# Moving the digit block of VectorE, the high digits of ScalarE and the gate of GpSimd's index cells in a product-key layer pipeline

## The reference

```python
h = h + attention(layernorm(h))          # scores, softmax and values all from the same rows
h = h + ffn(layernorm(h))
# ffn, for each token and each of 8 heads:
q = layernorm(hidden @ Wq.T + bq) * ln_g + ln_b       # 64 values, two halves of 32
s0, s1 = l2norm(q0) @ l2norm(keys0).T, l2norm(q1) @ l2norm(keys1).T   # 64 scores each
sc0, ix0 = top_k(s0, 16); sc1, ix1 = top_k(s1, 16)
cs = sc0[:, None] + sc1[None, :]; ci = ix0[:, None] + ix1[None, :]    # 256 candidates
fs, pos = top_k(cs, 16); fi = ci[pos]; w = softmax(fs)
out = sum over heads and 16 picks of gelu(hidden . down[fi]) * w * up[fi]
```

## Time and profile before

| | |
|---|---|
| time, median of 3 runs | 2086.8 us (2083.2 to 2092.77) |
| profiled execution, its own time | 2086.99 us |
| its span | 2085.2 us |
| its mean granted TensorE clock | 0.77 |
| busy: PE, DVE, ACT, POOL | 1701.8, 1925.5, 1217.5, 1554.2 us |

### The profile page before, as it was taken

The page is one execution under the profiler, slowest core; times in us unless marked ns, Lnnn a source line. Parts: engine busy times, 40 slices in busy tenths (PEclk is TensorE's granted clock), DMA queues, the critical chain, the costliest instruction groups (busy, mean ns, idle before and its releaser), DMA issues.

```text
span 2085.2 us, 48099 instructions
## 1 busy us (share of the span) xinstructions
PE 1701.8 (82%) x11423; PEld 1296.2 (62%) x11423; DVE 1925.5 (92%) x15878; ACT 1217.5 (58%) x3851; POOL 1554.2 (75%) x2561
## 2 busy tenths in 40 slices
PE   5567888888889898898888898888988989788766
PEld 3335576756767576675667667565765757566556
DVE  3299999999999999999999999999999999999992
ACT  3345656666565566655566665666665556665454
POOL 2238787886878788787878868788787767878765
PEclk9676878768787777877788678876878777787666
DMA  1000000000000000000000000000000000000000
GB/s 35 13 9 2 19 7 8 20 6 19 6 19 7 6 19 9 19 6 18 8 6 19 9 17 9 13 12 6 19 7 19 9 9 16 7 13 9 6 6 11
DMA packets 46672, 24.86 MB, mean 12 GB/s; under 512 B 4955, under 2 KB 46116, under 8 KB 46390
## 3 DMA queue, kind: packets, MB, share of 16 engines
q1 hardware_dynamic: 46390, 21.80, 3.7%
HBM read 11.52 MB, written 10.26 MB: 10 GB/s over the span
## 4 chain that ended last, share of the span: by engine, by line
PE 38%; DVE 30%; ACT 16%; POOL 9%; issue 5%; SPq 0%; another core or an unknown queue 0%; DMA 0%; POOLq 0%; DVEq 0%; ACTq 0%
PE QB L531 8%; DVE alpha L1046 5%; PE FB L449 5%; PE FB L440 4%; PE SC L480 4%; ACT WD L732 4%; DVE idx L1030 4%; DVE idx L1033 4%; DVE hrest L1024 3%; PE QB L519 3%; ACT hi L672 3%; PE FB L421 3%; DVE vals L1028 2%; DVE vals L1021 2%; POOL sa L762 2%
## 5 line engine op out<-in xcount | busy, mean ns | idle before, releaser
L892 POOL TENSOR_TENSOR bw<-beta,wp 128x1024 bf16<-128x1024 bf16 x240 | 508.1, 2148 | 117.2 <-ACT wp L718 117.2
L531 PE MATMUL QB<-bw,alpha 128*128 128x48 bf16 x5120 | 555.0, 278 | 32.2 <-issue 32.2
L531 PEld LDWEIGHTS QB<-bw,alpha 128*128 128x128 bf16 x5120 | 523.1, 151 | 73.9 <-issue 65.5
L732 ACT ACTIVATE WD<-QB 32x96 f32<-32x96 f32 x1280 | 307.7, 240 | 76.4 <-PE QB L531 65.1
L1046 DVE TENSOR_SCALAR alpha<-hi 128x1024 bf16<-128x1024 bf16 x640 | 276.0, 501 | 0.0
L480 PE MATMUL SC<-WK,hidT 128*128 128x512 f32 x320 | 223.2, 787 | 50.6 <-ACT stdT L664 43.7
L1030 DVE FIND_INDEX8 idx<-vals,sraw 128x8 uint32<-128x64 f32 x1280 | 250.9, 219 | 0.0
L1033 DVE FIND_INDEX8 idx<-vals,hrest 128x8 uint32<-128x64 f32 x1280 | 250.7, 220 | 0.0
L1024 DVE MATCH_REPLACE8 hrest<-vals,sraw 128x64 f32<-128x64 f32 x1280 | 249.6, 208 | 0.0
L840 POOL TENSOR_TENSOR ci<-idxf 128x64 f32<-128x64 f32 (+3 forms) x400 | 124.3, 347 | 135.8 <-DVE beta L1052 135.6
L725 ACT ACTIVATE ofin<-QB 128x128 f32<-128x128 f32 x80 | 22.2, 278 | 281.0 <-PE QB L531 278.3
(11 more groups left out here) (205 smaller groups left out, 3963.5 us busy)
## 6 DMA issues: line engine op xcount, KB each, us to landing
res<-h_scratch SPq DMA_DIRECT2D x80, 64.0 KB, 1.8
xin<-in_x SPq DMA_DIRECT2D x32, 128.0 KB
h_scratch<-h2n SPq DMA_DIRECT2D x32, 128.0 KB
out<-ofin SPq DMA_DIRECT2D x64, 64.0 KB, 1.5
h_scratch<-h2n SPq DMA_DIRECT2D x32, 28.5 KB
out<-ofin SPq DMA_DIRECT2D x16, 57.0 KB
xin<-in_x SPq DMA_DIRECT2D x32, 28.0 KB
xin<-in_x SPq DMA_DIRECT2D x32, 0.2 KB
```

The costliest lines, as they stand in the source:

```text
L531: last = mm(bank[:, 48 * u:48 * u + 48], alpha[:, buf, a, :, 8 * p + u], bwv[:, :, a, :, 8 * p + u], start=(a == 0), stop=(a == 1))
L732: last = A(WD[r, RING[(t - 4) % NT], :, 8 * p:8 * p + 8], blocks[r, :, :, g], ACT.Copy)
L892: last = tt(bw[:, buf, NY * i:NY * i + NY, :], beta[:, buf, :, :], wp[:, buf, i, :].unsqueeze(1).to_broadcast([128, NY, 256]), ALU.mult)
```

## The change

On ACT, hi moves from the head of part 0 to the place behind the first weight part and idxf. On POOL, ci no longer waits for beta_full. On DVE, the digit block leaves part 1 and stands in part 2 between the two index searches; zs and rz, and the front piece behind part 1, thereby come directly after MATCH_REPLACE8. In slots past the last tile it stands alone in part 2. norms moves from part 1 to the end of part 2.

```diff
--- before.py
+++ after.py
@@ -665,12 +665,6 @@
 
             def slot(k, t, p):
                 n = NT * k + t
-                if p == 0 and exists(k, t, 3):
-                    act.wait_ge(s["eb_full"], n - 2)
-                    after(act, s["alpha_full"], n - 3)
-                    for c in range(NS):
-                        last = A(hi[:, c, :], STE, ACT.Identity, bias=cdig[:, c:c + 1])
-                    last.then_inc(s["his_full"], 1)
                 if p == 0 and exists(k, t, 2):
                     buf = RING[(t - 2) % NT]
                     act.wait_ge(s["c2_full"], n - 1)
@@ -697,6 +691,12 @@
                     act.wait_ge(s["halves_full"], n)
                     after(act, s["ci_full"], n - 1)
                     A(idxf[:], idx[:, buf, :, :], ACT.Identity, bias=cquart[:]).then_inc(s["idxf_full"], 1)
+                if p == 0 and exists(k, t, 3):
+                    act.wait_ge(s["eb_full"], n - 2)
+                    after(act, s["alpha_full"], n - 3)
+                    for c in range(NS):
+                        last = A(hi[:, c, :], STE, ACT.Identity, bias=cdig[:, c:c + 1])
+                    last.then_inc(s["his_full"], 1)
                 if p == 0 and t == NT - 1 and exists(k, 0, 0):
                     act.wait_ge(s["inner_full"], k + 1)
                     A(GLn[:, 0:480], SC[:, 0:480], ACT.Gelu)
@@ -868,8 +868,6 @@
                     newton(y4[:], xh4[:], na[:], c15[:], s["rn_steps"], 12 * k, rn[:])
                 if p == 1 and exists(k, t, 1):
                     buf = RING[(t - 1) % NT]
-                    if exists(k, t, 3):
-                        pool.wait_ge(s["beta_full"], n - 2)
                     pool.wait_ge(s["idxf_full"], n)
                     cells(ci[:, buf, :, :], idxf[:], s["ci_full"])
                 if p == 2 and exists(k, t, 2):
@@ -1002,6 +1000,26 @@
                 dve.wait_ge(s["n2_steps"], 2 * j + 2)
                 seed(n2[:], xh4[:], y4[:], s["seed4_full"])
 
+            def digits(k, t):
+                n = NT * k + t
+                if exists(k, t, 3):
+                    old = RING[(t - 3) % NT]
+                    dve.wait_ge(s["his_full"], n - 2)
+                    after(dve, s["beta_full"], n - 3)
+                    V.scalar_tensor_tensor(out=lo[:], in0=STE, scalar=BASE, in1=hi[:, 0, :], op0=ALU.add, op1=ALU.subtract
+                                           ).then_inc(s["lo_full"], 1)
+                    after(dve, s["quads_full"], 4 * (n - 4))
+                    h8 = hi[:].rearrange("p c (m q) -> p c m q", q=NQ)
+                    a8 = alpha[:, old, :, :, :].rearrange("p a (g c x) q -> p c (a g) x q", g=NG, c=NS)
+                    for xx in range(NX // NS):
+                        last = V.tensor_scalar(a8[:, :, :, xx, :], h8, BASE + float(NY * xx), None, ALU.is_equal)
+                    last.then_inc(s["alpha_full"], 1)
+                    after(dve, s["bw_full"], n - 4)
+                    dve.wait_ge(s["lo_full"], n - 2)
+                    for y in range(NY):
+                        last = V.tensor_scalar(beta[:, old, y, :], lo[:], y - 1.5, None, ALU.is_equal)
+                    last.then_inc(s["beta_full"], 1)
+
             def slot(k, t, p):
                 n = NT * k + t
                 if p == 0 and exists(k, t, 0):
@@ -1028,31 +1046,17 @@
                             V.max(vals[:, buf, i, 8:16], rest[i]).then_inc(chain, 1)
                         for i in range(16):
                             V.max_index(idx[:, buf, i, 0:8], vals[:, buf, i, 0:8], raw[i]).then_inc(chain, 1)
+                        digits(k, t)
                         for i in range(16):
                             dve.wait_ge(chain, 32 + i + 1)
                             last = V.max_index(idx[:, buf, i, 8:16], vals[:, buf, i, 8:16], rest[i])
                             last.then_inc(chain if i < 15 else s["halves_full"], 1)
+                if p == 2 and not exists(k, t, 0):
+                    digits(k, t)
+                if p == 2 and t == NT - 1 and exists(k, t, -1):
+                    norms(k + 1)
                 if p == 1:
-                    digits, sums = exists(k, t, 3), exists(k, t, 2)
-                    old = RING[(t - 3) % NT]
-                    if digits:
-                        dve.wait_ge(s["his_full"], n - 2)
-                        V.scalar_tensor_tensor(out=lo[:], in0=STE, scalar=BASE, in1=hi[:, 0, :], op0=ALU.add, op1=ALU.subtract
-                                               ).then_inc(s["lo_full"], 1)
-                        after(dve, s["quads_full"], 4 * (n - 4))
-                        h8 = hi[:].rearrange("p c (m q) -> p c m q", q=NQ)
-                        a8 = alpha[:, old, :, :, :].rearrange("p a (g c x) q -> p c (a g) x q", g=NG, c=NS)
-                        for xx in range(NX // NS):
-                            last = V.tensor_scalar(a8[:, :, :, xx, :], h8, BASE + float(NY * xx), None, ALU.is_equal)
-                        last.then_inc(s["alpha_full"], 1)
-                    if digits:
-                        after(dve, s["bw_full"], n - 4)
-                        dve.wait_ge(s["lo_full"], n - 2)
-                        for y in range(NY):
-                            last = V.tensor_scalar(beta[:, old, y, :], lo[:], y - 1.5, None, ALU.is_equal)
-                        last.then_inc(s["beta_full"], 1)
-                    if t == NT - 1 and exists(k, t, -1):
-                        norms(k + 1)
+                    sums = exists(k, t, 2)
                     if sums:
                         dve.wait_ge(s["cand_chain"], 31)
                         dve.sem_clear(s["cand_chain"])
```

## The result

The changed kernel takes 2177.5 us (median of four runs, 2172.4 to 2186.9) where the kernel before, on the same chip, takes 2086.3: a ratio of 1.0438, 95% interval 1.0389 to 1.0487. It is slower, as forecast, but by 91 us where the forecast said 22, and lies outside the range. The profiled run has a span of 2180.3 us, 95 more than before.

A forecast was written before the change was run, and what follows sets the result against it. DVE sets the pace, with a ring of PE, ACT and POOL nearly as tight. (2.15 - 0.3) x 14 pairs = +26, -2.6 for norms' wait, -1 in the last tiles: 2087 + 22 = 2109 us, range 2059 to 2133.

The forecast's parts named there:

- Step (4): Tile 2: DVE's row seed for the residual newly waits 1.4 us for ACT's sums of squares, delaying DVE's work behind it.
- (5): Tile 2: alpha takes turns with POOL's wz, Yw and Ye, costing 3.05 us; ends 0 and 3.6.
- step (6): Tile 2's later candidate search delays zexp, so ACT enters tile 3 2.15 us later, all passed on.
- Step (7): Tile 0: with ci ungated, PE's wait for POOL's Ye gains 0.3 us a pair; ends +1.7 and -1.8.
- Step (3): Norms behind the second index search: the first pair's single 2.6 us wait goes, -2.6 us once.
- Step (2): DVE: lo's 22.6 us wait for hi goes; zs needs zexp instead, put at 1 us a pair of DVE time.
- Step (8): Other tiles' digit blocks: excess 1.5 us in tile 4, some 2 in tile 0, about 0 to 0.6 in 1 and 3.
- Rival (c): DVE becomes slower than the PE, ACT and POOL ring, four blocks a pair meeting Yw and Ye: 2162 us, chance 0.10.
- Step (9): Drain: lo waits for less, but bw may meet a block; 0, ends -3.3 and +3.3.

The follow-up runs named there:

- e1: The changed kernel, but in tile 2 of each pair POOL's wz (Yw and Ye behind it) waits for beta; 2143.4 us, ratio 1.0266.
- e9: The changed kernel with POOL's fourth Newton chain moved from tile 0 to tile 1; 2183.4 us, ratio 1.0455.
- e17: The changed kernel with norms between the index searches ahead of the digits, and POOL's wz waiting for beta in tiles 2 and 4; 2135.7 us.
- e14: The kernel before with norms alone moved behind the second index search; 2136.7 us, ratio 1.0235.
- e13: The changed kernel with norms moved to right behind the first index search, ahead of the digits; 2190.2 us, ratio 1.0476.

## Why the prediction was wrong

The direction holds, and so do the place and the mechanism of steps (4) to (6) for tile 2: the seed's new wait, wz ahead of alpha, 3.04 us of turns for 3.05, ACT's entry at A+26.4 for A+26.05, tile 2 longer by 2.37 us for 2.15. That term of the sum, 30 us, measured 33, and e1 gave back 34. (The durations of step (6) add up to A+26.2 and not A+26.05; that is 2 us in all.) The sum failed in the tiles around it. Tile 0 cost 1.60 us a pair, 22 us, where the sum had a gain of 0.3. Tile 3 cost 1.53, 21 us, and tiles 4 and 1 together 1.04, 15 us, where it had nothing.

**Step (7) is the term that was mis-sized most.** It put PE's wait for Ye in tile 0 at 0.3 us a pair less. It went from 1.7 us to 3.3 (46.3/14), 1.6 more, and that is what tile 0 grew by. The step had named this end itself, "-1.8 if POOL is held through a block", and POOL is held: by the block of tile 0 for 3.05 us in 11 pairs, and by the block of tile 4, where the five cs sums take 4.7 us in 13 pairs instead of 1.5. The range did not follow from the step either. With (7) at -1.8 the sum is 2087 + (2.15 + 1.8) x 14 - 3.6 = 2139, and with (5) at 3.6 as well 2146; the prediction gives 2125 for these two ends, and its range stops at 2133. What no run shows is that this term could be had back by itself: in e9 the wait falls by two fifths, and tiles 2 and 3 take its place.

**Step (6)** says "I pass on all of it", and for tile 3 that was too little. After ACT's late entry into tile 3, PE's next matmuls wait for squares queued behind it, and PE comes out of that wait at half the clock. The kernel before, then the changed one:
```profile
1130.76 1.32 PE L440 MATMUL FB<-hidTn,WcT 128*128 128x313 f32 x4 [1.51 <-ACT sq L653]
```
```profile
1187.21 2.46 PE L440 MATMUL FB<-hidTn,WcT 128*128 128x313 f32 x4 [3.55 <-ACT sq L653]
```
The granted clock around them (last columns: clock, DMA share, GB/s) was 1.00 before and 0.66 after, with 0.50 over the four matmuls themselves:
```profile
1129.70:1133.70 4.00, 2.94 (x9) 1.63 (x10) 3.97 (x19) 3.45 (x10) 1.08 (x5) 1.00 0.00 0
```
```profile
1186.20:1191.20 5.00, 3.99 (x8) 2.33 (x9) 4.96 (x45) 3.31 (x10) 3.26 (x3) 0.66 0.01 2
```
It is so in every steady pair: 1.32 us for the four before, 2.45 after. Those four matmuls and ACT's squares take turns, so the 1.1 us are on the path: the scores of tile 3 start 7.3 us behind ACT's entry instead of 6.1, and the first of them are 0.4 us slower. From there to the end of the tile the two kernels agree, so this is all of tile 3's 1.53. The prediction had no term for it. No run takes it away by itself. In e1 and e17 ACT enters tile 3 in time and the tile stays as long, for there PE waits for bw, late behind the gate, and comes out of that wait at 0.50 too.

**Tile 4's 0.61 us** are a cover lost. Step (6) saw that hi no longer covers zexp's wait; it did not ask what hi had covered behind zexp. With hi gone from the head, ACT reaches its first weight part 1.3 us sooner and finds PE still at the transposes into U:
```profile
1079.17 1.22 PE L487 MATMUL U<-ident,Yw 128*128 128x128 f32 x4
...
1081.88 0.38 ACT L681 ACTIVATE wp<-U 128x256 bf16<-128x256 f32 x1 [0.76 <-PE U L491]
```
Scores start at 9.0 us for 8.1 to 8.3. The 1.22 us are at half the clock in every steady pair; in the kernel before this is so in every second pair (0.71 us in the others), and there hi covers it both times. e6, hi's late place alone, has the same 0.76 us wait and scores at 9.0.

**Step (3)** overlooked norms: "norms moves behind the second index search. The single 2.6 us wait of the first pair goes: -2.6 us, once." It asked what norms waits for and not what stands beside it. The rows to ask were at hand: POOL's Ye and bw of the earlier trace rows are the long products, and the second search of tile 4 ends where they run. e14 prices the move at +49 us in the kernel before. In the changed kernel it is 43 us of DVE's time, but not of the kernel's: DVE's tile 4 is as long as before (26.3 us for 26.4, its block now 4.1 us for 6.0), ACT comes later still, and e17 gains nothing from having it away. That it did no harm here is luck: the other terms were worse.

**Step (4)** was right in kind and half the size, 1.4 us for 3.1 (39.8/13). I had read one pair. In the kernel before the lag from DVE's start of tile 2 to ACT's entry alternates from pair to pair, 0.7 and 3.5 us over all the steady pairs, and the pair of the earlier trace rows is one of those with 0.7. With 3.5 the same working gives 4.2 us, and the mean of both, 2.8, is within 0.3 us of what came. The sum did not suffer, since steps (5) and (6) count from ACT's entry and not from DVE's arrival.

**Step (2)** took zexp's cover at 1 us a pair and in DVE's slack; it is 3.1 (43.1/14). **Step (8)** was too high for the blocks of tiles 0 and 4 (3.6 and 4.1 us, an excess of 0 and 0.4 for 2 and 1.5) and too low for tile 1 (4.9 us). **Rival (c)** came nearest in time, 2162, but its four blocks beside Yw and Ye did not occur; only tile 2's did. Step (9) and the single wait of step (3) are too small to see.

**What stays open.** After e17, 48 us remain. Counted from the table reload, its tiles 3 and 4 are 1.8 us longer each than before and tile 0 is 0.7 shorter. Tile 3 is the wait for bw that the gate brings; for tile 4 no run isolates a cause. e6 shows that hi's late place lengthens tile 4 by 1.2 us and tile 0 by 1.5 when nothing else is changed. Whether hi at the head would recover them in e17's form was not tried; in the changed kernel itself it did not (e3), and there the blocks fell into POOL's products again (alpha 334.6 us).

## What to carry to other kernels

Before moving short instructions of one engine, list what the engine that shares its path to memory is doing at the new place, for every moved instruction and not only for the big block: in e14 four instructions of 0.25 us, moved alone, cost more than half of what the whole change costs. Then ask who is last at the new place: in the changed kernel the same instructions, 43 us longer, cost DVE's time and, as far as the runs tell, not the kernel's. Read a periodic kernel over two periods at least, since a lag can alternate. Where a change makes PE wait in front of a chain that PE and another engine walk in turns, look up the same matmuls at the lower clock and give the difference a term. And carry the ends of each term through to the range.

## What the runs showed of the hardware that was not expected

**Who was in flight first decided who paid.** POOL's product of six elements, which takes 0.20 us alone, began 0.10 us behind the first alpha instruction in tile 0 of the changed kernel and was held through the whole block (the row shows its first six alpha instructions):
```profile
1114.14 2.09 DVE L1015 TENSOR_SCALAR alpha<-hi 128x1024 bf16<-128x1024 bf16 x6
1114.24 3.25 POOL L762 TENSOR_TENSOR sa<-sy 128x6 f32<-128x6 f32 x1
```
The block lost nothing (3.63 us), and POOL 3.05. In tile 2 POOL was first by 0.56 us and the two took turns: the first three alpha instructions took 0.63, 1.32 and 2.33 us and ended with wz, Yw and Ye, the other five 0.41 each. DVE lost 3.04 us and POOL little (Yw 1.17 for 1.10, Ye 2.29 for 2.13). How much a small shift can do is seen in e13, where a block that begins 1 us later in tile 4 takes 3.9 us more.

**PE at half the clock over the same rows.** The five microseconds around ACT's entry into tile 4 have the granted clock at 1.00 in this pair of the kernel before and at 0.50, the lower of the two levels (1.2 of 2.4 GHz), in the changed one:
```profile
1029.80:1034.80 5.00, 4.76 (x75) 4.15 (x72) 4.22 (x25) 4.92 (x15) 4.30 (x12) 1.00 0.12 31
```
```profile
1079.00:1084.00 5.00, 5.00 (x55) 3.70 (x50) 4.96 (x47) 4.18 (x13) 4.28 (x13) 0.50 0.11 30
```
The kernel before alternates here too: in the next pair (1151.3 to 1156.3 us) the clock is 0.58, and the slow transposes of the section above stand in every second pair. In the changed kernel it is 0.50 in all of them. Over the whole run the mean falls only from 0.770 to 0.748, but PE's busy time rises by 64 us, and part of it lies where ACT waits for each result.
